# First stage's last group worked batch by batch, its one-hot matrices made earlier, and a context transpose given two more PSUM banks

## The chip, the cores and the metric

The kernel runs on one NeuronCore of a Trainium2 chip. The metric is the device time of one execution in microseconds (us). PE is TensorE, DVE is VectorE, ACT is ScalarE, POOL is GpSimd and SP is SyncE. PE's sequencer, like each of the others, takes its instructions in the order in which the program has them, so an instruction that waits for a semaphore holds up all that stand behind it on that engine.

## The reference, cut to what matters

Six layers, each followed by a residual addition and a layer norm, on 8 batches of 256 tokens of 256 features:

```python
x = _layernorm(x + L0_attn(x))            # 16 heads of 64, causal
x = _layernorm(x + L0_xattn(x, ctx))      # one head, 120 context rows, weights = softmax(q @ ctx.T + mask)
x = _layernorm(x + L0_ffn(x))             # 8 experts, the best 2 of each token, softmax of the 2 gates
x = _layernorm(x + L1_attn(x))            # 16 heads of 16, gated, then an MLP
x = _layernorm(x + L1_xattn(x, ctx))      # 4 heads of 64 on 120 context rows
x = _layernorm(x + L1_ffn(x))             # token shift, receptance, squared relu
```

## The kernel before, in words

A "tile" is 128 tokens. The 16 tiles are worked in G = 4 groups g of NT = 4 tiles, that is GB = 2 batches of 256 tokens. SBUF is one tensor (`words` in the profile) and PSUM another (`bank`, 8 banks of 512 floats), so the profile's names tell a space only; lines tell the operation. Order and semaphores are written by hand for each engine. There are three blocks of code with a barrier between them.

**First stage** (`attention_layers`, lines 165 to 771): the first attention, the first context attention, the gate and the routing. A group has 16 units (batch, pair of heads), and each unit goes round the engines: scores on PE (`unit_scores`, L369), maximum on DVE (L691, L695), exponential on ACT (L571), reciprocal of the sum on DVE (L700), multiplication on POOL (L324), transposes on PE (`unit_turn`, L382) three units later, copy on DVE (L706), value product on PE (`unit_heads`, L395) four units later, copy to `zt` on ACT (L579). Then comes the group's tail: output product (L505, four tiles), residual and statistics (L709, L108, L110), the power on POOL (L128, L130, `norm_rstd`), the normalised rows (L120), their transposes (L406, copied by ACT L559), query product (`tail_queries`, L414), logits (L425), maximum (L723), exponential (L591), transposes of the weights (L435), context sums (L443), the same statistics and rows again for the second norm, its transposes, the gate product (`tail_gate`, L452), the choice of the two experts on DVE (L739 to L748, `choose` L620 to L626), the count on PE (`count`, L462, L463, L466) and the rank in the expert's list (`rank`, L634 to L647). For groups 0 to 2 this tail is interleaved with the projection of the next group (`project`, L358). Group 3 has no next group, and its tail stands alone.

**Table of sources.** Every (tile, choice) pair n = 0 to 31 has two one-hot matrices of 128x128, the "low" (L313) and the "high" (L315), made by POOL from the ranks (`one_hot`), the last eight high ones by DVE (L765). PE multiplies each pair into one accumulating bank (`place`, L477). There are OH = 8 buffers, which lie over the buffers of the unit loop, so that none is made before the last unit of group 3 is done. From the count DVE also works out columns (`columns`, L653 to L675), and a last product (L540) gives the list of rows per slot tile (L771). The three first experts' weights are loaded by SP when the last unit has left (`load_expert`); the rest in the second stage.

**Second stage** (`expert_layer`, to line 1003): 39 slot tiles. POOL gathers the rows (L829) and copies half the expert's up weights (L842), ACT copies the other half (`copy_weights`, L935) and the transposed rows (`copy_rows`, L920) and takes the sigmoid (L924). PE transposes (L870), multiplies up (L886) and down (L897).

**Last stage** (`last_layers`): the three last layers as a pipeline of periods. In period p the front works group a = p, the middle r = p - 1, the rear z = p - 2; periods 2 and 3 have all three. In the rear, `context_turn` (L1424) transposes the softmaxed context weights of a tile into a bank, `context_copy` (L1937, ACT) takes them out, `context_sums` (L1435, copied by ACT L1981) multiplies by the values, `context_product` (L1335, banks 6 and 7 by turns) is added by DVE (`add_product`, L2343). All `product` calls have line 1335. In the periods `context_turn` used bank 1 for all four tiles:

```python
def context_turn(g, t, banks=(1,), sm=sm):
    if t >= len(banks):
        pe.wait_ge(xtc, NT * g + t - len(banks) + 1)
```

## Time and profile before

| | us |
|---|---|
| median of 3 runs | 1292.29 (1290.97 to 1292.76) |
| the profiled execution's own time | 1291.66 |
| its span, from the first to the last instruction | 1289.9 |
| PE busy in the span | 1125.7 (87%) |
| DVE busy | 743.0 (58%) |
| ACT busy | 543.1 (42%) |
| POOL busy | 456.0 (35%) |
| mean granted TensorE clock | 0.951 of full speed |

All positions below are us from the span's start. The first stage ends at about 522, the second at about 750. A time line's row has the start, the time from the first start to the last end of the merged instructions, engine, line and operation, the output and its inputs, the number of records (a float32 product is two records on PE), and in brackets how long the engine had been idle before and what released it.

### The profile page before, as it was taken

What the parts mean: (1) busy time and instruction counts of PE and PEld (TensorE: products, weight loads), DVE (VectorE), ACT (ScalarE), POOL (GpSimd) and SP (SyncE); (2) the same over time, 40 slices, a digit from 0 to 9 for tenths busy, and PEclk for the clock granted to TensorE, in tenths of its full rate; (3) what the DMA queues carried; (4) which work ended last, traced back from release to release, by engine and by line L of the source; (5) the groups of instructions that cost most, each with busy time, mean ns of one, the idle gap of its engine ahead of it and who ended that gap; (6) DMA issues with size and microseconds to landing.
All of it is one profiled execution on the core that took longest, in us unless ns stands there. A gap on an engine that the chain in (4) does not pass through costs nothing. (4 is left out here: it accounts for less than half of the span.)

```text
span 1289.9 us, 20369 instructions
## 1 busy us (share of the span) xinstructions
PE 1125.7 (87%) x6738; PEld 794.2 (62%) x6738; DVE 743.0 (58%) x2247; ACT 543.1 (42%) x1409; POOL 456.0 (35%) x531
## 2 busy tenths in 40 slices
PE   7889988998899886799999937788898898889996
PEld 3456446644654565799999925554654575466775
DVE  1482376347524844455656536758748577756366
ACT  1371246126421721233333317466465457443541
POOL 0150035004300557666666541524322422232122
PEclk9999999999999998799999969589998999899998
DMA  6000110020001040651111132100000100000001
GB/s 194 17 1 1 46 27 2 1 56 17 1 1 56 2 158 19 221 182 51 50 50 47 43 119 64 33 1 25 10 8 1 34 9 17 1 1 25 1 1 33
DMA packets 40228, 52.38 MB, mean 41 GB/s; under 512 B 10780, under 2 KB 33372, under 8 KB 40124
## 3 DMA queue, kind: packets, MB, share of 16 engines
q1 hardware_dynamic: 31100, 36.66, 8.9%
q0 software_dynamic: 3408, 9.31, 2.6%
q10 hardware_dynamic: 5616, 5.11, 1.2%
q8 instruction: 55, 0.90, 0.3%
q14 instruction: 49, 0.40, 0.1%
HBM read 41.76 MB, written 9.31 MB: 40 GB/s over the span
## 5 line engine op out<-in xcount | busy, mean ns | idle before, releaser
L1335 PE MATMUL bank<-words 128*128 128x256 f32 (+3 forms) x872 | 275.4, 467 | 20.9 <-ACT words L1921 5.7
L1335 PEld LDWEIGHTS bank<-words 128*128 128x128 f32 (+1 forms) x872 | 164.8, 196 | 105.5 <-issue 58.9
L358 PE MATMUL bank<-words 128*128 128x512 f32 x384 | 172.7, 601 | 8.3 <-DMA words<-in_wq 8.3
L324 POOL TENSOR_TENSOR words<-words 128x256 f32<-128x256 f32 (+1 forms) x128 | 103.6, 831 | 189.9 <-DVE words L700 189.9
L886 PEld LDWEIGHTS bank<-words 128*128 128x128 f32 x1248 | 147.6, 194 | 4.3 <-ACT words L920 2.4
L886 PE MATMUL bank<-words 128*128 128x128 f32 x1248 | 148.1, 278 | 1.7 <-ACT words L920 1.7
L571 ACT ACTIVATE words<-words 128x128 f32<-128x128 f32 (+1 forms) x256 | 113.3, 444 | 50.0 <-DVE words L695 50.0
L358 PEld LDWEIGHTS bank<-words 128*128 128x128 f32 x384 | 72.3, 192 | 90.4 <-issue 89.8
L553 ACT ACTIVATE words<-bank 128x512 f32<-128x512 f32 x48 | 28.7, 598 | 192.1 <-PE bank L358 192.1
L935 ACT ACTIVATE words<-words 128x1024 f32 x39 | 41.2, 1057 | 146.3 <-PE bank L886 120.8
L610 DVE COPY words<-bank 128x512 f32<-128x512 f32 x48 | 33.2, 691 | 105.8 <-PE bank L358 105.6
L691 DVE CUSTOM_DVE_ANT_0 words<-bank,words 128x128 f32<-128x128 f32 (+1 forms) x256 | 76.0, 354 | 20.5 <-PE bank L369 18.9
L897 PE MATMUL bank<-words 128*128 x312 | 73.9, 380 | 0.7 <-DVE words L984 0.7
L382 PE MATMUL bank<-words 128*128 128x128 f32 x384 | 55.8, 282 | 16.8 <-DVE words L706 9.1
L369 PE MATMUL bank<-words 64*128 64x128 f32 (+1 forms) x512 | 58.9, 351 | 8.6 <-DVE words L695 5.2
L395 PE MATMUL bank<-words 128*64 128x256 f32 (+1 forms) x512 | 55.7, 337 | 10.5 <-ACT words L579 9.4
L382 PEld LDWEIGHTS bank<-words 128*128 128x128 f32 x384 | 41.5, 143 | 38.0 <-issue 30.3
L706 DVE COPY words<-bank 128x768 f32<-128x768 f32 x64 | 59.7, 932 | 8.3 <-PE bank L382 8.3
L1228 POOL TENSOR_TENSOR words<-words 128x2 f32<-128x2 f32 x32 | 7.0, 218 | 162.0 <-DVE words L2353 161.9
L842 POOL COPY words<-words 128x1024 f32 x39 | 40.4, 1037 | 61.4 <-PE bank L886 61.4
L1993 ACT ACTIVATE words<-bank 128x768 f32<-128x768 f32 x64 | 48.9, 811 | 29.3 <-DVE bank L2445 29.2
L128 POOL TENSOR_TENSOR words<-words 128x4 f32<-128x4 f32 x8 | 1.6, 203 | 167.3 <-DVE words L110 167.3
(301 smaller groups left out, 2051.2 us busy)
## 6 DMA issues: line engine op xcount, KB each, us to landing
words<-in_w SPq DMA_DIRECT2D x8, 1024.0 KB, 12.3
y_slots<-words ACTq DMA_DIRECT2D x39, 128.0 KB, 1.7
words<-in_w SPq DMA_DIRECT2D x8, 512.0 KB, 12.6
words<-in_xt SPq DMA_DIRECT2D x4, 512.0 KB, 3.7
words<-in_x SPq DMA_DIRECT2D x4, 512.0 KB, 4.2
x_rows<-words SPq DMA_DIRECT2D x16, 128.0 KB, 1.8
words<-in_wm SPq DMA_DIRECT2D x2, 1024.0 KB, 6.5
out_x<-words SPq DMA_DIRECT2D x16, 128.0 KB, 1.8
```

Source lines behind the costliest of these rows:

```text
L324: last = pool.tensor_tensor(part, part, inv[:, j % SLOTS0, :, t:t + 1].to_broadcast([P, 2, P * (t + 1)]), ALU.mult)
L358: last = pe.matmul(bank[c % 2][:, :], w, r, start=k == 0, stop=k == KD - 1)
L369: last = pe.matmul(bank[SCORES[i % 2][n]][:, t * P:t * P + P * (t + 1)],  kt[r, m, b * S + t * P:b * S + (t + 1) * P], qt[r, m, b * S:b * ...
L382: last = pe.transpose(bank[2 + n][:, k * P:(k + 1) * P], prob[:, j % SLOTS0, n, c:c + P], ident[:, :])
L395: last = pe.matmul(bank[4 + j % 2][DH0 * n:DH0 * n + DH0, queries], v[:, 2 * b + k, h * DH0:(h + 1) * DH0], probt[:, j % 2, n, probs_of], ...
L571: last = act.activation(prob[:, i % SLOTS0, n, c], prob[:, i % SLOTS0, n, c], ACT.Exp, bias=negmax[:, i % SLOTS0, n, t:t + 1], scale=DH0 * ...
L691: dve.tensor_tensor_reduce(out=prob[:, i % SLOTS0, n, c], in0=bank[SCORES[i % 2][n]][:, c], in1=mask0[:, c], scale=1.0, scalar=-3e38, op0= ...
L706: dve.tensor_copy(probt[:, j % 2, :, :], turned).then_inc(tcopied, 1)
L886: last = pe.matmul(bank[(BANKG, BANKV)[half][j % 2]][:, c * P:(c + 1) * P], wfix[:, j % 2, k * 2 * FF + half * FF + c * P:k * 2 * FF + hal ...
L897: last = pe.matmul(bank[BANKY[j % 2]][:, 0:D], hidden[:, j % 2, k * P:(k + 1) * P], w2[:, bass.ds(e * W2 + k * D, D)], start=k == 0, stop= ...
L1335: last = pe.matmul(out, w, r, start=i == 0, stop=i == len(pairs) - 1)
L1993: act.activation(es[:, j % 4, :, :], pair(j % 2)[:, :, 0:CAUSAL], ACT.Exp, scale=DH1 ** -0.5).then_inc(s1e, 1)
```

## The change

Four things are changed.

1. The last group's tail in the first stage is worked by batches of two tiles, b = 0 and 1, with functions of its own on each engine (`last_output`, `last_turn`, `last_queries` and so on). Two of the four output products and the first transposes stand inside the end of the unit loop; the steps of batch 0 stand between those of batch 1.
2. The one-hot matrices get more room: 4 of the 32 pairs in a buffer of their own (`firsthots`), 8 over `wv` (free once the last projection is done), 4 over `xt`, and 8 (`latehots`) over the unit loop's buffers. POOL makes the first four in group 2's units (one in four units), the next eight in group 3's (one in two units). The last count is split in two, so 4 pairs instead of 8 depend on it alone. Since expert 2's weights lie over `wv`, their load waits for the 12th placement and stands behind the stores of the group's rows on SP.
3. In the second stage ACT copies the second slot tile's weights before the first tile's rows, no longer after the first sigmoid.
4. In periods 2 and 3 of the last stage the context weights of tiles 2 and 3 are transposed into banks 6 and 7, after the fourth query/key product; the first two MLP products (`up`) stand ahead of the four context sums, no longer between them.

```diff
+        latehots = cut(turning, 0, (OH, 2, P))
+        firsthots = sb([P, OH // 2, 2, P])
+        weighthots = wv[:, :, :].rearrange("p k (h r n) -> p (k h) r n", r=2, n=P)
+        tokenhots = xt[:, :, :].rearrange("p k (h r n) -> p (k h) r n", r=2, n=P)
...
-                    for e in range(EARLY):
+                    for e in range(EARLY - 1):
                         load_expert(sp, dram, keep, e)
...
+            sp.wait_ge(placed, OH + OH // 2)
+            load_expert(sp, dram, keep, EARLY - 1)
             sp.wait_ge(rowsout, 16 * NT * G)
...
+                    if g == FINAL - 1 and j % 4 == 0:
+                        pool.wait_ge(ranked, 1)
+                        one_hot(j // 4)
+                    if g == FINAL and j % 2 == 0:
+                        pool.wait_ge(ranked, 2)
+                        one_hot(OH // 2 + j // 2)
...
+            one_hot(OH + 4)
+            one_hot(OH + 5)
+            last_rstd(n1, 0)
+            one_hot(OH + 6)
+            one_hot(OH + 7)
+            pool.wait_ge(ranked, G - 1)
+            pool.wait_ge(heads, UNITS * G)
+            for n in range(2 * OH, 2 * OH + 6):
                 one_hot(n)
+            last_rstd(n1, 1)
+            one_hot(2 * OH + 6)
+            one_hot(2 * OH + 7)
+            last_rstd(n2, 0)
+            last_rstd(n2, 1)
             pool.wait_ge(ranked, G)
-            for n in range(3 * OH, 4 * OH):
+            for n in range(3 * OH, 3 * OH + OH // 2):
+                one_hot(n)
+            pool.wait_ge(ranked, G + 1)
+            for n in range(3 * OH + OH // 2, 4 * OH):
                 one_hot(n, both_parts=False)
...
+                    if g == FINAL and i == UNITS:
+                        pe.wait_ge(zcopied, UNITS * g + PAIRS0)
+                        pe.wait_ge(shifted, UNITS * g + UNITS - 1)
+                        last_output(0)
+                        last_output(1)
+                    if g == FINAL and i == UNITS + 2:
+                        pe.wait_ge(shifted, UNITS * g + UNITS)
+                        last_turn(n1, 0, lambda t: x1[:, t, :], TURNED1[0])
...
+            last_queries(0)
+            pe.wait_ge(zcopied, UNITS * G)
+            pe.wait_ge(tcopied, UNITS * G)
+            last_output(2)
+            pe.wait_ge(loaded, 16 * LOADS * G)
+            last_logits(0)
+            last_output(3)
+            last_weights(0)
+            last_sums(0)
+            place(0, OH)
+            last_turn(n1, 1, lambda t: x1[:, t, :], TURNED1[1])
+            place(OH, OH + OH // 2)
+            last_queries(1)
+            last_logits(1)
+            last_turn(n2, 0, lambda t: x2(FINAL, t), TURNED2[0])
+            last_gate(0)
+            last_weights(1)
+            last_sums(1)
+            place(OH + OH // 2, 2 * OH)
+            last_count(0)
+            place(2 * OH, 3 * OH)
+            last_turn(n2, 1, lambda t: x2(FINAL, t), TURNED2[1])
+            last_gate(1)
+            last_count(1)
+            place(3 * OH, 4 * OH)
...
+            last_output(2)
+            last_max(0)
+            last_output(3)
+            last_rows(n1, 1, lambda t: x1[:, t, :])
+            last_sums(0)
+            last_rows(n2, 0, lambda t: x2(FINAL, t))
+            last_max(1)
+            last_gate(0)
+            choose(FINAL, 0)
+            last_sums(1)
+            rank(FINAL, 0)
+            last_rows(n2, 1, lambda t: x2(FINAL, t))
+            last_shares(0)
+            last_gate(1)
+            choose(FINAL, 1)
+            rank(FINAL, 1)
+            for n in range(4 * OH - OH // 2, 4 * OH):
...
             copy_weights(0)
+            copy_weights(1)
             copy_rows(0)
             sigmoid(0)
-            copy_weights(1)
             copy_rows(1)
...
                 if z is not None:
-                    context_turn(z, 2)
-                    context_turn(z, 3)
-                    pe.wait_ge(xtc, NT * z + NT)
+                    pe.wait_ge(xtc, NT * z + HALF)
                 if a is not None:
                     queries_keys(a, 3)
...
                 if z is not None:
                     pe.wait_ge(xe, GB * z + GB)
-                for q in range(GB * KD):
-                    if z is not None:
+                    context_turn(z, 2, (6, 7))
+                    context_turn(z, 3, (6, 7))
+                if r is not None:
+                    for c in range(2):
+                        pe.wait_ge(vcop, NT * a + c + 3)
+                        up(r, c)
+                if z is not None:
+                    pe.wait_ge(xtc, NT * z + NT)
+                    for q in range(GB * KD):
                         context_sums(z, q)
```

PE at the end of the first stage before: the last value products of the unit loop (L395), all four output products (L505), then each step for four tiles.

```order
L395 MATMUL bank<-words 64x128 x2
L505 MATMUL bank<-words 128x256 x32
L477 MATMUL bank<-words 128x128 x8
L406 MATMUL bank<-words 128x128 x8
L414 MATMUL bank<-words 128x512 x4
L425 MATMUL bank<-words 128x120 x8
L435 MATMUL bank<-words 120x128 x4
```

PE at the same place in the changed kernel, from the last value product of the loop (L456). L558 is the query product, L542 an output product, L567 logits, L575 transposes of weights, L582 context sums, L535 placements, L550 row transposes.

```order
L456 MATMUL bank<-words 64x128 x2
L558 MATMUL bank<-words 128x256 x4
L542 MATMUL bank<-words 128x256 x8
L567 MATMUL bank<-words 128x120 x4
L542 MATMUL bank<-words 128x256 x8
L575 MATMUL bank<-words 120x128 x2
L582 MATMUL bank<-words 128x256 x2
L535 MATMUL bank<-words 128x128 x8
L550 MATMUL bank<-words 128x128 x4
L535 MATMUL bank<-words 128x128 x4
L558 MATMUL bank<-words 128x256 x4
```

Batch 0 has its queries, logits, weights and sums between the output products of batch 1, and the first 12 placements stand around the transposes of batch 1.

PE in the context attention of period 2 before: transposes (L1424), the products (L1335, of which the 512-wide pair ahead of the first sums is the fourth query/key product and the next two are `up`), sums (L1435).

```order
L1335 MATMUL bank<-words 128x512 x2
L1335 MATMUL bank<-words 128x256 x4
L1424 MATMUL bank<-words 120x128 x8
L1335 MATMUL bank<-words 128x512 x2
L1435 MATMUL bank<-words 64x128 x4
L1335 MATMUL bank<-words 128x512 x2
L1435 MATMUL bank<-words 64x128 x4
L1335 MATMUL bank<-words 128x512 x2
L1435 MATMUL bank<-words 64x128 x8
```

The same place in the changed kernel (L1631 products, L1720 transposes, L1731 sums):

```order
L1631 MATMUL bank<-words 128x256 x4
L1631 MATMUL bank<-words 128x512 x2
L1720 MATMUL bank<-words 120x128 x8
L1631 MATMUL bank<-words 128x512 x4
L1731 MATMUL bank<-words 64x128 x16
```

The fourth query/key product has moved ahead of the last two transposes, and all four sums stand together behind both `up` products.

## Rows read from the trace of the kernel before

**Rows 1.** Windows view: stretch, length, PE, PEld, DVE, ACT, POOL busy, PEclk, DMA.

```profile
466.60:522.30 55.70, 43.67 (x204) 35.15 (x204) 24.25 (x102) 6.77 (x23) 40.80 (x60) 0.84 0.30 102
```

**Rows 2.** Time line of PE, end of the first stage.

```profile
457.90 0.87 PE L395 MATMUL bank<-words 128*64 128x256 f32 x8
...
467.03 14.08 PE L505 MATMUL bank<-words 128*128 128x256 f32 x64 [0.48 <-ACT words L579]
...
480.95 1.95 PE L477 MATMUL bank<-words 128*128 128x128 f32 x16
...
486.58 3.70 PE L414 MATMUL bank<-words 128*128 128x512 f32 x8 [0.47 <-ACT words L559]
...
491.18 1.12 PE L425 MATMUL bank<-words 128*128 128x120 f32 x8 [0.89 <-issue]
...
504.83 3.25 PE L452 MATMUL bank<-words 128*128 128x8 f32 x16
```

**Rows 3.** Time line of DVE, end of the first stage.

```profile
500.00 0.45 DVE L733 SCALAR_TENSOR_TENSOR words<-bank,words 128x256 f32<-128x256 f32 x1
...
501.04 0.18 DVE L110 BATCH_NORM_AGGREGATE words<-words 128x2 f32<-128x6 f32 x1
...
502.72 1.44 DVE L120 TENSOR_SCALAR words<-words 128x256 f32<-128x256 f32 x4 [1.50 <-POOL words L130]
...
508.11 0.19 DVE L739 COPY words<-bank 128x32 f32<-128x32 f32 x1 [3.95 <-PE bank L452]
...
513.17 0.28 DVE L634 TENSOR_TENSOR words<-words,bank 128x32 f32<-128x32 f32 x2 [0.87 <-PE bank L466]
...
514.94 2.44 DVE L765 TENSOR_SCALAR words<-words 128x128 f32<-128x128 f32 x8
...
522.07 0.20 DVE L771 CAST words<-bank 128x39 int32<-128x39 f32 x1 [0.74 <-PE bank L540]
```

**Rows 4.** Time line of POOL, units of group 3 and a one-hot.

```profile
447.75 1.62 POOL L324 TENSOR_TENSOR words<-words 128x256 f32<-128x256 f32 x2 [1.45 <-DVE words L700]
...
450.22 1.62 POOL L324 TENSOR_TENSOR words<-words 128x256 f32<-128x256 f32 x2 [0.85 <-DVE words L700]
...
503.32 1.02 POOL L315 TENSOR_SCALAR words<-words 128x128 f32<-128x128 f32 x1
```

**Rows 5.** Groups by line, POOL's one-hots: busy us, mean ns, idle before.

```profile
L313 POOL TENSOR_SCALAR words<-words 128x128 f32<-128x128 f32 x32 | 19.6, 619 | 5.3 <-PE bank L395 4.3 <-DVEq L648 1.0
...
L315 POOL TENSOR_SCALAR words<-words 128x128 f32<-128x128 f32 x24 | 19.5, 814 | 0.0
```

**Rows 6.** Time lines of PE and ACT at the start of the second stage.

```profile
535.12 3.84 PE L886 MATMUL bank<-words 128*128 128x128 f32 x32 [1.25 <-ACT words L920]
...
533.74 1.06 ACT L935 ACTIVATE words<-words 128x1024 f32 x1 [0.17 <-issue]
```

**Rows 7.** Time line of PE, context attention of periods 2 and 3.

```profile
977.35 0.65 PE L1424 MATMUL bank<-words 128*120 128x128 f32 x4 [1.75 <-DVE words L2410]
...
980.09 3.78 PE L1335 MATMUL bank<-words 128*128 128x512 f32 x4 [0.69 <-ACT words L1937]
...
1001.43 3.71 PE L1335 MATMUL bank<-words 128*128 128x512 f32 x8 [2.67 <-ACT words L1921]
...
1121.86 5.40 PE L1335 MATMUL bank<-words 128*128 128x512 f32 x8 [2.99 <-ACT words L1921]
```

**Rows 8.** Time line of DVE, the same stretches.

```profile
989.61 1.34 DVE L2648 TENSOR_SCALAR words<-words 128x128 f32<-128x128 f32 x1
...
992.84 0.42 DVE L2343 TENSOR_TENSOR words<-bank,words 128x256 f32<-128x256 f32 x1 [1.89 <-PE bank L1335]
...
1112.95 0.42 DVE L2343 TENSOR_TENSOR words<-bank,words 128x256 f32<-128x256 f32 x1 [1.73 <-PE bank L1335]
```

**Rows 9.** Windows view while PE ran the rows at 980.09 and 1121.86.

```profile
980.00:982.00 2.00, 1.91 (x3) 0.87 (x4) 2.00 (x2) 0.04 (x1) 0.50 (x1) 0.50 0.00 0
...
1124.00:1128.00 4.00, 4.00 (x14) 1.92 (x13) 0.00 (x0) 0.27 (x1) 0.00 (x0) 0.72 0.00 0
```

More of the change, by code:

```diff
@@ L469, in place @@
-            def place(first, number=OH):
-                for n in range(first, first + number):
+                pe.matmul(bank[3][:, 0:NT * NE], ones[:, :], running[:, NT * g:NT * (g + 1), :].rearrange("p t e -> p (t e)"),
+                          start=False, stop=True).then_inc(counted, 1)
+            def place(first, last):
+                for n in range(first, last):
                     pe.wait_ge(hotlow, n + 1)
-                    if n < 3 * OH:
+                    if n < 4 * OH - OH // 2:
@@ L651, in columns @@
             def columns():
[L653 removed]
+                dve.tensor_scalar(length[:, :], bank[SUMMED[1]][:, HALF0 * NE:HALF0 * NE + NE], (P - 1) / 2, 1 / P, ALU.add, ALU.mult)
                 dve.drain()
@@ new lines, in last_shares @@
+            def last_shares(b):
+                h, tiles = slice(HALF0 * b, HALF0 * b + HALF0), slice(NT * FINAL + HALF0 * b, NT * FINAL + HALF0 * b + HALF0)
+                first, second = (keep["weight"][:, tiles, r] for r in range(2))
+                dve.wait_ge(gexp, FINAL + b + 1)
+                dve.tensor_scalar(gq[:, h], ge[:, h], 1.0, None, ALU.add)
+                dve.drain()
+                dve.reciprocal(first, gq[:, h])
+                dve.drain()
+                dve.tensor_tensor(second, first, ge[:, h], ALU.mult)
```

281 lines of the change are left out of this document (215 added, 66 removed).

## Prediction

> **What bounds the kernel now.** All positions are us of the profiled execution, whose span is 1289.9 and whose own time is 1291.66, 0.63 under the median of the three runs, 1292.29. I read the windows view first, to see where no engine is full, then the time lines of PE, DVE and POOL there, for who waits for whom. From the last value product of the first stage to its end lie 55.7 us [rows 1]. PE is busy for 43.67 of them and POOL for 40.80, neither is full, and the granted clock averages 0.84. It is a serial chain: 14.08 us of output products before any normalised row can be turned, then a chain of steps each of which takes four tiles [rows 2, 3]. That chain is the first place of the change.
>
> The second is the start of the second stage, where PE waits 1.25 us for ACT, which was in a 1.06 us weight copy [rows 6].
>
> The third is the context attention of periods 2 and 3. PE shows gaps around its transposes, but DVE works without a gap up to the end of L2648 (989.61 + 1.34 = 990.95) and only then waits, 1.89 us for the first context product, in period 3 1.73 us [rows 7, 8]. Since DVE's next result feeds ACT's last exponential, its table load and the gelu for which PE waits at 1001.43, this DVE wait bounds the place, not PE's gaps.
>
> **End of the first stage.** The work is the same but for order, so I walk the new order with the old durations.
>
> PE leaves the heads of the twelfth unit at 457.90 + 0.87 = 458.8 [rows 2]. Now two output products of 14.08 / 4 = 3.52 each follow, to 465.8, in time that used to be the loop's draining. Then come seven steps of units (three turns, four heads) of 0.87 each, eight turn records (about 1.0) and some 0.5 of waits for DVE's copies: 473.4. Queries for one batch cost 3.70 / 2 = 1.85, output product three 3.5, logits of one batch 1.1 (the row at 491.18 is for two tiles), the last output product 3.5 [rows 2]. It ends at 483.4, while before it ended at 467.03 + 14.08 = 481.1.
>
> From there to the last statistics of the second norm took 20.1 before (481.1 to 501.04 + 0.18 = 501.2) for four tiles. For two tiles I take off 1.85 of queries, 0.7 of turning, 1.3 of the four maxima and exponentials, and 2.3 for two of the four statistics, which stand 1.2 apart (500.00 to 501.22) [rows 3]: 14.0. I add what now stands between: up to 2.0 for placements (eight take 1.95 [rows 2]) and context sums ahead of batch 1's turn, 0.9 for the turn and gate of batch 0 on PE, 0.8 for gate and choice of batch 0 on DVE. That makes 17.7, so 501.1: by then nothing has been won, since the later output products have eaten it.
>
> After that the halves pay. Before, from 501.2: 1.50 for POOL's power, rows at 502.72, gate on DVE at 508.11, the count read at 513.17, high one-hots 514.94 to 517.38, end at 522.07 + 0.20 = 522.27 [rows 3]. Now DVE ranks batch 0 while POOL works, to 502.9; two rows (half of 1.44), one turn, one copy and a gate product of 3.25 / 2 = 1.6 (at the low clock of that row; about 1.0 at the high one) bring the gate to 506.2, so 1.9 less. Gate and choice handle half the width: 0.7 less. The count saves 0 to 0.7 by the clock; I take 0.2. Four high one-hots instead of eight save half of 2.44, 1.2. Columns, table and last product stay. The sum is 4.0: **the stage ends at 518.3**. Bounds: 3.2 if the clock is low all along, 4.9 if it stays high, and 1.5 more or less for the 501.1.
>
> POOL's one-hots: a pair costs 0.62 + 0.81 = 1.43 [rows 5]. Twelve pairs move into the units. Two units use 2 x 1.62 of POOL and leave 1.45 + 0.85 idle, a period of 5.54 [rows 4]; with one pair more POOL is at 4.67 of it. After a pair the next multiplication can be late by 1.43 - 0.85 = 0.58, but PE reads it only three units after its scores, so I cost it at nothing. If that cover were gone, see the rivals. Pairs 12 to 23 are made while POOL would wait: the six before the second power of the first norm (8.6 us from the heads at 473.4) end near 482, and tile 3's statistics come at 484.6. Expert 2's load now starts near 504, behind two row stores on SP, and is not used before the slot tiles of experts 0 and 1 are done, so it costs nothing.
>
> **Second stage.** ACT copies the second tile's weights before the rows arrive, when it is idle. The row copy that PE waits for then starts right behind PE's transposes instead of behind the rest of a 1.06 us copy [rows 6]. Of the 1.25 us wait some 0.45 remain for the row copy itself: 0.8 won. Nothing, if ACT's copy were late for the first rows, is the lower bound.
>
> **Context attention.** PE no longer waits between transposes 977.35 and 980.09 [rows 7], and the first context product is ready by about 987. DVE then starts at 990.95, and 1.89 and 1.73 are the most that can be won [rows 8]. But PE, ahead by then, idles some four us, since the third product waits for DVE's first addition. The row at 980.09 shows what follows short work with gaps: four records take 3.78, where eight take 3.71 in the row at 1001.43, and the granted clock is 0.50 [rows 7, 9]. If the clock falls to its lower level (1.2 GHz of 2.4) at that point, products three and four are late by about 1.2 and `up` by more, and 0.5 of the 1.89 remains. In period 3 the same fall now hits the two `up` products behind the gelu: 5.40 where period 2 has 3.71, at a granted clock of 0.72 [rows 7, 9]; with PE busy before, that 1.7 should go. So 0.5 and 0.5 + 1.7: **2.7 us**; between 0 and 3.6 + 1.7.
>
> The Trainium skill (TensorE: Matmul & The Clock Gate, What's actually happening) states that the clock is passed at one of two ratios, set by how busy PE has been recently. The granted 0.50 and the row of 3.78 agree; by that rule a PE that gets ahead and then idles loses part of its lead, and by the row alone I would have taken the full 3.6.
>
> **Sum.** 4.0 + 0.8 + 2.7 = 7.5. Against the median: 1292.3 - 7.5 = **1284.8**.
>
> **Rivals.**
> - *The clock holds.* PE stays at the high level through the end of the first stage (+0.9) and the context products (+0.9). For: PE is denser than before in both. Against: 0.84 in the stretch before [rows 1], and PE still waits for DVE. 9.3 won, 1283.0.
> - *Interleaving costs more.* Each engine runs both batches in one queue, so one late step of batch 0 (its rows wait for POOL, its gate for PE) holds batch 1. If three such waits of 1 us hit the chain, the first stage gives 1.0 and the whole 4.5: 1287.8. For: DVE has 16 steps of the two batches in one queue. Against: I found each input ready but for about 1 us.
> - *The context part gives nothing*, because PE's lost clock eats it: 4.8 won, 1287.5.
> - *One-hots hold the units: slower.* They share POOL with the multiplications on which the turns rest. It decides where a one-hot pair takes over 5.54 - 3.24 = 2.30 us, or where PE's turns have no slack for 0.58. If all of 12 x 1.43 = 17.2 lay on the path, the kernel would lose 9.7: 1302. For: POOL's high one-hot took 1.02 when DVE's row scaling ran beside it, 0.81 on average [rows 4, 5]. Against: even then a pair is 1.7.
>
>   The Trainium skill (SBUF — State Buffer, Who interferes with whom) has a rule that speaks against this: GpSimd and a VectorE instruction of a two-port mode take turns on one port pair, and the later one waits for the whole instruction. By it, DVE's small scalings between units would be held by up to a one-hot each, 12 x 0.81 = 9.7, and the kernel would be 2.2 slower if none of that were hidden. The trace agrees only with a wait on POOL's side: DVE's four rows took 1.44 beside the slowed one-hots [rows 3, 4].
>
> **Chances.** Forecast 0.50, clock holds 0.20, interleaving 0.14, context nothing 0.08, one-hots hold the units 0.04, the rest (an expert's load or a barrier that hides all) 0.04. 0.2%, 2.6 us, is about what a measurement of this kernel can tell from no change. The first four, 0.92, are all faster by more, and I take 0.02 off for small gains; 0.06 for within and 0.04 for slower. The range reaches from the clock rival with the upper bound of the context part (1292.3 - 11 = 1281.3) to the interleaving rival with the ACT term gone (1292.3 - 3.5 = 1288.8).
>
> **What would show it.** The last CAST of the first stage at 518.3 instead of 522.07 + 0.20, with the last statistics of the second norm near 501 and the last output product's end near 483.4; the unit loop's period unchanged at 5.54 per two units and no PE wait for POOL's L371; no wait of PE before the second slot tile's products above 0.5; DVE's first context addition directly behind its scaling of the squares in periods 2 and 3, and the gelu release 0.5 to 1.9 us earlier in the stage's own time. It would be wrong if the units' period grew, if the chain between 483 and 501 took over 20, or if periods 2 and 3 kept their length.

## The result, and the profile after

The changed kernel takes 1287.22 us (median of 20 runs, 1281.88 to 1293.22), the kernel before 1292.5 us (20 runs, 1290.67 to 1296.24). The ratio is 0.9955, its 95% interval 0.9945 to 0.9965: **5.8 us faster, 4.5 to 7.1**. The profiled execution took 1288.51 us, with a span of 1286.8 and a mean granted clock of 0.949, against 0.951 before.

**End of the first stage.** Time line of PE in the changed kernel, as in [rows 2]. L542 is an output product, L550 a transpose, L558 the query product, L535 a placement, L590 the gate:

```profile
460.12 7.17 PE L542 MATMUL bank<-words 128*128 128x256 f32 x32
...
480.46 3.63 PE L542 MATMUL bank<-words 128*128 128x256 f32 x16
...
485.75 1.95 PE L535 MATMUL bank<-words 128*128 128x128 f32 x16
487.53 0.60 PE L550 MATMUL bank<-words 128*128 128x128 f32 x4
...
503.83 1.06 PE L590 MATMUL bank<-words 128*128 128x8 f32 x8 [0.69 <-ACT words L718]
```

The two early output products stand inside the unit loop, and the last one ends at 480.46 + 3.63 = 484.1. Time line of DVE, as in [rows 3]: rows of the first norm of batch 1, last statistics of the second norm, high one-hots, end of the stage.

```profile
486.51 0.79 DVE L899 TENSOR_SCALAR words<-words 128x256 f32<-128x256 f32 x2 [1.19 <-POOL words L363]
...
500.05 0.18 DVE L882 BATCH_NORM_AGGREGATE words<-words 128x2 f32<-128x6 f32 x1
...
510.57 1.28 DVE L1060 TENSOR_SCALAR words<-words 128x128 f32<-128x128 f32 x4
...
516.84 0.20 DVE L1067 CAST words<-bank 128x39 int32<-128x39 f32 x1 [0.19 <-PE bank L693]
```

The stage ends at 517.04, 5.2 before the 522.27 of [rows 3]. But group 3's units began at 418.69 in this execution and at 417.67 in the one before: the first unit began 1.19 earlier here, but group 0 then took 2.08 longer, in code that both kernels share. From there to the end it took 104.60 before and takes 98.35: **6.25 won in the tail**. In the time frame of the kernel before, 1.02 is to be taken off every position above.

These are two single executions, and the one before was a quick one. Two experiments below (ACT's order only, context part only) have the old code in this stage, and it took 106.85 and 106.86 in their profiles. The first difference is the query product, 3.70 before [rows 2], here in ACT's order only:

```profile
486.09 5.40 PE L414 MATMUL bank<-words 128*128 128x512 f32 x8 [0.47 <-ACT words L559]
```

The new code took 98.1 to 99.2 in the eight profiles that have it without a change to its one-hots. So the tail wins between 5.4 and 8.8 us by profiles.

**Units with one-hots in them.** Groups by line, PE's transposes from the start of group 3's units to the last heads (about 56 us), first the kernel before, then the changed one:

```profile
L382 PE MATMUL bank<-words 128*128 128x128 f32 x96 | 13.8, 280 | 4.7 <-DVE words L706 2.6 <-POOL words L324 1.5
```

```profile
L443 PE MATMUL bank<-words 128*128 128x128 f32 x96 | 13.7, 279 | 4.5 <-DVE words L983 2.6 <-POOL words L371 1.5
```

The wait for POOL's multiplications is 1.5 us with and without one-hots between them. The units are a little slower all the same: from the first score product of group 3 to its last it is 39.12 us before and in the three experiments without one-hots there, and 39.5 in the changed kernel and in the seven others with eight pairs. In the changed kernel two units take 5.88 instead of 5.53 at one place, and 5.53 from there on.

**Start of the second stage**, time line of PE, as in [rows 6]: L1166 transposes the gathered rows, L1182 multiplies up.

```profile
522.28 5.90 PE L1182 MATMUL bank<-words 128*128 128x128 f32 x32 [0.47 <-ACT words L1216]
...
528.88 3.84 PE L1182 MATMUL bank<-words 128*128 128x128 f32 x32 [0.47 <-ACT words L1216]
534.05 0.44 PE L1166 MATMUL bank<-words 128*128 128x128 f32 x2 [1.33 <-DMA words<-x_rows,words]
```

ACT's wait fell from 1.25 to 0.47, as forecast. Behind it a new one of 1.33 appeared, for the gathered rows of the third slot tile. From the end of the first stage to the third tile's transposes it is 534.05 - 517.04 = 17.0 us, and it was 538.80 - 522.27 = 16.5 before: this stretch became 0.5 longer.

**Context attention**, time line of PE, as in [rows 7]: the first two context products, then the third and fourth (8 records of 256 columns, merged in the second row with the 8 records of `up` 2 and 3), then the two `up` products behind the gelu, in period 2 and in period 3.

```profile
985.00 1.99 PE L1631 MATMUL bank<-words 128*128 128x256 f32 x8 [0.47 <-ACT words L2277]
991.57 8.44 PE L1631 MATMUL bank<-words 128*128 128x256 f32 x16 [4.57 <-DVE words L2639]
1001.14 3.71 PE L1631 MATMUL bank<-words 128*128 128x512 f32 x8 [1.13 <-ACT words L2217]
...
1121.26 3.71 PE L1631 MATMUL bank<-words 128*128 128x512 f32 x8 [1.46 <-ACT words L2217]
```

DVE's first and fourth context additions of period 2 and the first of period 3, as in [rows 8]:

```profile
991.11 0.41 DVE L2639 TENSOR_TENSOR words<-bank,words 128x256 f32<-128x256 f32 x1
...
995.39 0.42 DVE L2639 TENSOR_TENSOR words<-bank,words 128x256 f32<-128x256 f32 x1 [0.76 <-PE bank L1631]
...
1111.22 0.41 DVE L2639 TENSOR_TENSOR words<-bank,words 128x256 f32<-128x256 f32 x1
```

DVE no longer waits for the first product. PE, ahead, idles 4.57 us and comes back slow. Windows view of those slices (all engines; the last three numbers are the granted clock and the DMA's share and rate):

```profile
990.00:994.00 4.00, 2.43 (x6) 1.98 (x7) 3.26 (x8) 2.63 (x5) 1.68 (x3) 0.61 0.00 0
994.00:998.00 4.00, 4.00 (x8) 2.08 (x7) 2.89 (x8) 1.12 (x2) 1.45 (x3) 0.54 0.00 0
```

**Where the rest is.** The same instruction can be found in every kernel's trace. The table is worked out from the time lines of DVE: how many us later than in the changed kernel an instruction starts, at six of the changed kernel's positions. 600 and 850 lie behind the start of the second stage and in the last stage's first period, 969 is the beginning of period 2's context attention, 1008 behind its gelu, 1128.5 the same in period 3. Where a number changes from one column to the next, time was lost or won between.

| profile of | 600 | 850 | 969 | 1008 | 1128.5 | 1280 |
|---|---|---|---|---|---|---|
| before | 4.7 | 3.5 | 0.1 | 0.3 | 2.3 | 3.1 |
| tail only | -1.1 | -2.2 | -2.8 | -1.9 | 0.1 | 0.0 |
| ACT's order only | 6.5 | 5.3 | 1.9 | 2.1 | 4.0 | 4.0 |
| context part only | 6.3 | 5.1 | 1.8 | 1.4 | 1.0 | 2.4 |
| up products between | -0.7 | -0.4 | -1.1 | -0.4 | -0.4 | 1.3 |
| kept warm | -1.8 | -3.2 | -6.5 | -6.3 | -7.8 | -7.8 |
| loads held | -0.8 | -2.2 | -5.6 | -5.6 | -6.3 | -4.7 |
| one-hots twice | 8.4 | 8.6 | 8.0 | 8.0 | 8.0 | 11.2 |
| one-hots late | 18.0 | 16.7 | 13.4 | 13.4 | 12.6 | 15.4 |
| gap filled | 1.3 | 1.0 | 0.9 | 1.1 | 1.3 | 2.9 |
| both filled | -2.0 | -3.5 | -6.9 | -8.3 | -9.4 | -9.4 |
| warm and held | -0.2 | -1.3 | -1.9 | -1.7 | -1.5 | 0.1 |

Against the changed kernel, "before" is 4.7 behind at 600 and level at 969: **4.6 us of the win were lost again in code that the change does not touch**, all of it between 840 and 970. The windows view shows what the clock did there, between 882 and 958. First the kernel before, then the changed one (PE's busy time, the granted clock and the DMA's share and rate), then tail only (busy time of all engines, then the same three):

```profile
898.00:902.00 4.00, 3.30 (x16) 0.63 0.36 100
...
926.00:930.00 4.00, 2.09 (x32) 0.72 0.00 0
930.00:934.00 4.00, 3.91 (x52) 1.00 0.00 0
```

```profile
894.00:898.00 4.00, 3.23 (x16) 0.66 0.36 103
898.00:902.00 4.00, 3.42 (x20) 0.50 0.39 117
...
926.00:930.00 4.00, 2.11 (x33) 0.93 0.00 0
930.00:934.00 4.00, 3.94 (x25) 0.65 0.00 0
```

```profile
918.00:922.00 4.00, 2.72 (x32) 1.52 (x32) 3.37 (x17) 1.16 (x3) 0.10 (x1) 0.69 0.00 0
922.00:926.00 4.00, 1.98 (x20) 1.41 (x24) 2.65 (x7) 1.75 (x3) 3.05 (x5) 0.50 0.00 0
926.00:930.00 4.00, 4.00 (x24) 2.85 (x16) 2.32 (x6) 2.16 (x4) 0.24 (x1) 0.53 0.00 0
```

Before, one slice has PE at work at a low clock (898 to 902), and the other low one, 926 to 930, is half idle. In the changed kernel there are three with PE at work, one of them at 0.50; in tail only PE is busy through 926 to 930 at 0.53. Not every execution of the new tail pays this: kept warm, loads held and both filled have the same code there (loads held but for one wait of SP), are 5.5 to 6.7 ahead of "before" at 600 and 5.7 to 7.0 at 969, and one-hots late loses nothing there either. The other six with the new tail (the changed kernel, tail only, up products between, gap filled, warm and held, one-hots twice) lose 2.9 to 4.6, and the two with the old tail nothing. The runs fit that: the changed kernel's 20 times lie between 1281.9 and 1293.2, twice the spread of before.

### The profile page after: what moved, and what is told of

It is laid out like the page before. It is cut to its first block and busy times, and to the rows that moved or that the text cites. A ratio compares the mean times of both kernels' runs of the same rounds, so it can differ in the third digit from the quotient of the medians.

```text
span 1286.8 us, 20425 instructions
## 1 busy us (share of the span) xinstructions
PE 1123.6 (87%) x6750; PEld 796.0 (62%) x6750; DVE 743.7 (58%) x2260; ACT 544.2 (42%) x1407; POOL 459.7 (36%) x539
## 5 line engine op out<-in xcount | busy, mean ns | idle before, releaser
L1631 PE MATMUL bank<-words 128*128 128x256 f32 (+3 forms) x872 | 276.1, 469 | 26.7 <-DVE words L2639 9.1
L1631 PEld LDWEIGHTS bank<-words 128*128 128x128 f32 (+1 forms) x872 | 166.7, 198 | 112.7 <-issue 58.0
L1182 PEld LDWEIGHTS bank<-words 128*128 128x128 f32 x1248 | 147.4, 194 | 3.5 <-ACT words L1216 1.6
L1182 PE MATMUL bank<-words 128*128 128x128 f32 x1248 | 147.9, 277 | 0.9 <-ACT words L1216 0.9
L808 DVE COPY words<-bank 128x512 f32<-128x512 f32 x48 | 33.2, 691 | 104.6 <-PE bank L419 104.3
L456 PE MATMUL bank<-words 128*64 128x256 f32 (+1 forms) x512 | 56.4, 340 | 10.0 <-ACT words L762 9.0
L2741 DVE TENSOR_TENSOR bank<-bank,words 128x512 f32<-128x512 f32 x64 | 42.0, 694 | 32.9 <-PE bank L1686 32.6
```

What stands on the lines that cost most here:

```text
L456: last = pe.matmul(bank[4 + j % 2][DH0 * n:DH0 * n + DH0, queries], v[:, 2 * b + k, h * DH0:(h + 1) * DH0], probt[:, j % 2, n, probs_of], ...
L1182: last = pe.matmul(bank[(BANKG, BANKV)[half][j % 2]][:, c * P:(c + 1) * P], wfix[:, j % 2, k * 2 * FF + half * FF + c * P:k * 2 * FF + hal ...
L1631: last = pe.matmul(out, w, r, start=i == 0, stop=i == len(pairs) - 1)
L2741: dve.tensor_tensor(diagonal, diagonal, mask1[:, :].unsqueeze(1).to_broadcast([P, 4, P]), ALU.min).then_inc(s1m, 1)
```

## Experiments

The ratios are against the kernel before, run on the same chip: 1293.47 us (25 runs) for the three parts and up products between, 1292.83 (18 runs) for kept warm, loads held and the two kernels with other one-hots, 1292.29 (13 runs) for gap filled, both filled and warm and held. A range behind a ratio is its 95% interval.

### The three parts, each alone

**Tail only**: the changed kernel with ACT's order and the context part put back.

> The kernel before with the batchwise end of the first stage, the early one-hots and expert 2's late load alone; ACT's order in the second stage and the context transposes are as before. In the profile of the whole change this stage ended 6.25 us earlier, counted from the start of group 3's units (98.35 against 104.60), where the prediction had 4.0. Theory: that is the tail's own and is kept to the end, so 98.3 to 98.4 from the units' start and 5.5 to 6.5 us less in all. Rival, that part of it is PE's clock falling luckily in that profile: 99.5 to 101 here, and 4 us or less in all. PE's wait for the third slot tile's rows (the gather) stays at 0 in both, as ACT's order is the old one.

Measured: 1288.69 us (7 runs), ratio 0.9963 (0.9949 to 0.9977), **4.8 won, 3.0 to 6.6**, which holds both the 5.5 to 6.5 of the theory and the rival's 4. From the units' start to the end of the stage its profile has 99.2, which is neither's. Its second stage missed the forecast too: the third tile's transposes wait 0.43 for the gather, with ACT's order still the old one, and the wait for ACT is 0.60 where it was 1.25. Its profile is 5.8 ahead of before at 600 and 5.7 at 850. By 1008 only 2.2 of that are left: the rest was lost in the last stage, whose code is the same in both.

**ACT's order only**: the kernel before with `copy_weights(1)` moved up.

> The kernel before with ACT's second weight copy ahead of its first row copy alone. In the profile of the whole change the second slot tile's products began 0.94 us earlier, but PE then waited 1.33 us for the rows of the third slot tile. Theory: the gather of the third tile is issued at the same time as before and lands about 8.7 us later, because the experts' loads fill the DMA engines, so whatever ACT wins is waited away there: 0 us, with a PE wait of about 0.9 before the third tile's transposes. Rival, that the wait belongs to the whole change (expert 2's load moved): 0.8 to 0.9 us less and no such wait.

Measured: 1292.95 us (11 runs), ratio 0.9992 (0.9984 to 1.0001): 1.0 won, between -0.1 and 2.1, so the times alone tell 0.8 from nothing as little as from twice as much. The time line of PE tells more:

```profile
536.11 3.84 PE L886 MATMUL bank<-words 128*128 128x128 f32 x32 [0.47 <-ACT words L920]
540.59 0.44 PE L870 MATMUL bank<-words 128*128 128x128 f32 x2 [0.64 <-DMA words<-x_rows,words]
```

The wait is 0.47 instead of 1.25, and the next transposes, which before followed without a gap, wait 0.64 for the gather. Against the frame of the units, the second tile's products came 0.8 earlier and the third's at the old place. What ACT gave, the gather took: from the end of the first stage to the third tile's transposes it is 16.55, and 16.53 before.

**Context part only**: the kernel before with the new PE order and banks of periods 2 and 3.

> The kernel before with the context transposes of tiles 2 and 3 in banks 6 and 7 alone. Prediction: DVE's first addition 1.89 and 1.73 us earlier in periods 2 and 3, most of it lost in period 2 because the clock falls while PE idles and the third and fourth products are late; in period 3 the products behind the gelu take 3.7 instead of 5.4. That gives 0 to 0.5 for period 2 and 2.2 for period 3, 2.2 to 2.7 in all. Rival, that the clock is not the cause: both periods keep 1.7 to 1.9, 3.6 in all.

Measured: 1289.7 us (10 runs), ratio 0.9976 (0.9967 to 0.9985), **3.1 won, 1.9 to 4.3**. By the table it is 1.6 to 1.8 behind "before" at 600, 850 and 969 (its units began 0.66 earlier, and the end of the first stage, with the old code and the query product of 5.40, then took 2.26 longer) and 0.7 ahead at 1280: 2.4 in its profile. The first addition of period 2 came 1.98 earlier against the instructions just ahead of it, the fourth only 0.55. The table's step from 969 to 1128.5 is +2.2 in "before" and -0.8 here, so 3.0 by then, some of which goes again at the end.

By their medians the three parts add to 4.8 + 1.0 + 3.1 = 8.9, and the whole gives 5.8; with half-widths of 1.8, 1.1 and 1.2 the intervals overlap.

### PE ahead and idle: can the context products be used better?

**Up products between**: in periods 2 and 3,

```diff
-                    for t in range(NT):
-                        context_product(z, t)
+                    context_product(z, 0)
+                    context_product(z, 1)
...
+                    up(r, 2)
+                    up(r, 3)
...
+                    context_product(z, 2)
+                    context_product(z, 3)
...
-                    for c in range(2, 6):
-                        up(r, c)
+                    up(r, 4)
+                    up(r, 5)
```

> The whole change, and in the periods with a context attention the MLP products up 2 and up 3 stand between the second and the third context product, where PE idles about four us for DVE's first addition. Theory: PE works through that time, the clock stays at its upper level, products three and four take under 1 us each, and period 2 keeps the whole 1.9 us of DVE's earlier start: 1.3 to 1.9 us less than the whole change, most of it in period 2. Rival, that DVE's additions are bound by something else: no change, or up to 1 us more because the third product now waits behind up 3.

Measured: 1289.71 us (9 runs), ratio 0.9967 (0.9954 to 0.9981), no better than the whole change, where 1.3 to 1.9 less was expected. DVE's additions came earlier, but PE then had nothing before the gelu:

```profile
990.42 1.99 PE L1631 MATMUL bank<-words 128*128 128x256 f32 x8 [1.13 <-DVE words L2645]
998.53 3.78 PE L1631 MATMUL bank<-words 128*128 128x512 f32 x4 [6.11 <-ACT words L2223]
```

Four records took 3.78 (and all eight 5.90) where eight take 3.71 in the changed kernel. The gap had only been moved.

**Kept warm**: the same, and behind the fourth context product four products of 512 columns whose result nobody reads (L1968).

```diff
+                    pe.wait_ge(turning, NT * a + NT)
+                    for i in range(4):
+                        pe.matmul(bank[3][:, :], wm1[:, 0, tok(i)], h5t[:, 0, :], start=True, stop=True)
```

> The order of ups_between (up 2 and up 3 ahead of the third context product) with four 512-wide products more behind the fourth context product, whose result nobody reads, in the time in which PE waits for the first gelu (6.11 us in ups_between in both periods). Theory, that PE's idle time there costs the clock: the two products behind the gelu take 3.7 us instead of 5.90 and 5.22, the added products (0.93 each at the upper level, 3.7 us) lie inside the wait, and the kernel is 2.5 to 4 us faster than ups_between, that is 1.5 to 3 us faster than the whole change. Rival, that the clock does not depend on PE's own work there: 5.2 to 5.9 as before and no gain, or a loss if the added products hold up 4.

Measured: 1281.23 us (7 runs, 1280.28 to 1291.44), ratio 0.9932 (0.9908 to 0.9955), 8.8 won. Periods 2 and 3:

```profile
986.86 3.60 PE L1968 MATMUL bank<-words 128*128 128x512 f32 x8
993.14 5.40 PE L1631 MATMUL bank<-words 128*128 128x512 f32 x8 [2.68 <-ACT words L2226]
```

```profile
1107.19 3.60 PE L1968 MATMUL bank<-words 128*128 128x512 f32 x8
1113.47 3.71 PE L1631 MATMUL bank<-words 128*128 128x512 f32 x8 [2.68 <-ACT words L2226]
```

The same filler and the same 2.68 of idle time gave a slow pair in one period and a quick one in the other. In the stage itself the table gives 1.3 us (from -6.5 to -7.8). The other 6.5 that its profile is ahead were there at 969, before the edit acts, so **the median of this kernel is better by more than the edit explains**: five of its seven runs lie at 1280.3 to 1282.8 and two at 1287.7 and 1291.4.

**Gap filled** puts those four products where PE idles 4.57 us in the changed kernel, between the second and the third context product, in the order of the change (into the bank of `up` 2). **Both filled** has them and three more ahead of the wait for the gelu.

> The whole change, with four products of 512 columns whose result nobody reads put between the second and the third context product of periods 2 and 3, where TensorE idles 4.57 us for VectorE's first addition. Theory (the clock falls in that gap): the third and fourth context products run at the high clock, VectorE's fourth addition comes about 1.4 us earlier against the first one (2.8 after it instead of 4.3) in both periods, so 2.8 won; but TensorE then idles some 2.7 us before the gelu and the two products behind it take 5.40 instead of 3.71, which gives 0 to 3.4 back. Total between 3 us faster than the whole change and the same. Rival (the gap costs nothing, the clock falls by itself): the products behind the gap are as slow as before, the additions stand where they stood, and the time is the whole change's.

Measured for gap filled: 1288.07 us (8 runs), ratio 0.9959 (0.9945 to 0.9974), the same as the whole change. Its time line of PE:

```profile
987.73 3.60 PE L1960 MATMUL bank<-words 128*128 128x512 f32 x8
992.46 5.43 PE L1631 MATMUL bank<-words 128*128 128x256 f32 x16 [1.13 <-DVE words L2644]
1000.57 5.40 PE L1631 MATMUL bank<-words 128*128 128x512 f32 x8 [2.68 <-ACT words L2222]
```

The same 16 records take 5.43 here and 8.44 in the changed kernel: that is what 4.57 of idle time cost, 3.0 us (in period 3 it is 5.43 and 8.11). DVE's fourth addition comes 2.83 behind the first, not 4.28. And PE, done sooner, idles 2.68 before the gelu, after which the `up` pair takes 5.40 and not 3.71. From 969 to 1128.5 the table moves by 0.4. Both halves of the theory are seen, and they cancel.

> As the kernel with the products in the gap, and three more such products ahead of the wait for the gelu. Theory: both idle stretches are filled, so the additions come 1.4 us earlier in each period and the products behind the gelu stay at 3.71: 2.8 us less than the whole change, about 1284.5, without the reordering of the up products. Rival (in the kernel kept warm the order of the up products made the gain, not the filling): no faster than the whole change, 1287, or slower by what the added products hold up.

Measured for both filled: 1281.54 us (6 runs, 1279.11 to 1287.47), ratio 0.9929 (0.9911 to 0.9947). Period 2:

```profile
984.71 5.43 PE L1631 MATMUL bank<-words 128*128 128x256 f32 x16 [1.14 <-DVE words L2648]
989.98 2.74 PE L1970 MATMUL bank<-words 128*128 128x512 f32 x6
992.83 3.71 PE L1631 MATMUL bank<-words 128*128 128x512 f32 x8
```

Neither is slow now, in both periods, and the table gives 2.5 from 969 to the end (-6.9 to -9.4), of the 2.8 expected. The median is 5.7 under the whole change's; the rest again lies before 969 in the profile, in code that both share. So one profile shows 2.5 us for the filling, and the runs a median of 1281.5 for this kernel, but not that the filling brings all of the difference.

### The third tile's gather

**Loads held**: SP waits with expert 3's weights until the first two gathers of buffer 0, that of the third tile with them, have landed.

```diff
                     sp.wait_ge(gathered[1], 16)
+                    sp.wait_ge(gathered[0], 32)
```

> The whole change, and SP issues the loads of experts 3 to 5 only after the third slot tile's rows have landed. Theory, that the experts' loads on the DMA engines make the third gather take 8.7 us: it lands some 3 to 5 us earlier, PE's wait of 1.33 us before the third tile's transposes goes, and the kernel is 1.0 to 1.4 us faster than the whole change. Rival, that POOL's issue of the gather is late (it follows two weight copies): the wait stays at 1.3 and nothing changes. A second risk is that the wait comes back at the fourth or fifth tile, whose gathers then meet the loads.

Measured: 1284.91 us (6 runs), ratio 0.9944 (0.9927 to 0.9962), 7.2 won. The third tile has no wait, the fourth a small one:

```profile
532.62 0.38 PE L1167 MATMUL bank<-words 128*128 128x128 f32 x2
...
538.74 0.44 PE L1167 MATMUL bank<-words 128*128 128x128 f32 x2 [0.43 <-DMA words<-x_rows,words]
```

In both kernels with the load held the third tile's wait is gone, and in all seven others with ACT's new order and the new tail it is there, so the load beside the gather is what delays it. But its size differs in the same code: 1.33 in the changed kernel, 1.92 in up products between, 2.54 in gap filled, 0.39 in kept warm and 0.41 in both filled. From the end of the first stage to the transposes of the last slot tile it is 214.8 us with the load held, 215.8 in the changed kernel, and 214.7 in kept warm and both filled, which hold nothing. So the 1.0 between the two profiles, and the 2.3 between the medians, are not shown to be the edit's.

**Warm and held** is kept warm with this edit.

> The kernel kept warm (up products between the context products, four products nobody reads ahead of the gelu) with expert 3's load held until the third tile's rows have landed. If the two savings stand in different places and add: 0.9 to 1.4 us less than the kernel kept warm, about 1280. Rival: the start of the second stage is eaten again before the stage ends by a change of the clock, no difference from it.

Measured: 1285.76 us (6 runs), ratio 0.9944 (0.9925 to 0.9964), **a miss**: the two did not add, and it is no faster than loads held alone. The third tile's wait is gone and the fourth's 0.43 is there. There was nothing to win by that: kept warm's own wait at the third tile was 0.39 in its profile. But both `up` pairs behind the gelu were slow, and from 600 to 969 its profile fell back by 2.9 against "before", where kept warm lost nothing. Its six runs lie in two clumps, 1282.7 to 1283.8 and 1287.8 to 1290.4.

### The one-hots in the units

**One-hots twice**: each of the eight pairs of group 3's units is made twice, with a wait between.

```diff
                         pool.wait_ge(ranked, 2)
+                        again(OH // 2 + j // 2)
+                        pool.drain()
                         one_hot(OH // 2 + j // 2)
```

> The whole change, and in the units of group 3 POOL makes each of the eight one-hot pairs twice. Theory: two units have 5.54 us, POOL needs 2 x 1.62 for them and 1.43 for a pair, and PE reads its result only later, so one pair is hidden (measured: the unit loop of group 3 is 0.4 us longer than before at most), but two are not: 3.24 + 2.86 = 6.10, so 0.56 us more for each of the eight double units, 3 to 5 us in all. Rival, that POOL has more slack than that or that DVE's small operations are held by each one-hot: 0, or over 8 us.

Measured: 1295.45 us (10 runs), ratio 1.0014 (1.0003 to 1.0024). POOL over one period of two units (L377 is the multiplication, L360 begins the extra pair and L352 the one that is kept), and PE's group of transposes:

```profile
446.24 3.19 POOL L377 TENSOR_TENSOR words<-words 128x256 f32<-128x256 f32 x4
449.40 0.61 POOL L360 TENSOR_SCALAR words<-words 128x128 f32<-128x128 f32 x1
...
450.95 0.60 POOL L352 TENSOR_SCALAR words<-words 128x128 f32<-128x128 f32 x1 [0.17 <-issue]
...
452.30 3.19 POOL L377 TENSOR_TENSOR words<-words 128x256 f32<-128x256 f32 x4
```

```profile
L451 PE MATMUL bank<-words 128*128 128x128 f32 x90 | 13.7, 291 | 9.0 <-POOL words L377 8.2 <-DVE words L991 0.8
```

POOL has next to no idle time left, the period is 452.30 - 446.24 = 6.06 instead of 5.53, and PE's wait for it grew from 1.5 to 8.2. The group's score products now take 43.2 us instead of 39.5, so 3.7 more in the loop. The forecast of 3 to 5 in all was missed: the whole lost 7.6 against the changed kernel by the ratios, and in the profiles the stage from the units' start was 7.2 longer (105.5 against 98.35), half of it behind the loop. One pair in two units is hidden but for the 0.4 of the section on the profile, two are not.

**One-hots late**: none is made before the last unit has left; the 24 that were early are made around the powers of the tail.

> The whole change with no one-hot matrix in the units: POOL makes all 24 pairs of groups 0 to 2 after the unit loop, between the powers of the norms. Theory: the batchwise order is only worth something with the early matrices. 24 x 1.43 = 34 us of POOL and four powers end about 512 instead of the last of the 24 at 489, and PE's placements of them stand ahead of the second norm's transposes of batch 1, so the stage ends 8 to 10 us later and the kernel is 2 to 5 us slower than the kernel before. Rival, that the matrices are hidden anyway as they were before: 0 to 2 us later than the whole change.

Measured: 1304.93 us (4 runs), ratio 1.0093 (1.0079 to 1.0108), 12.0 slower than before and some 18 slower than the whole change. PE (L529 is a placement, L544 a row transpose):

```profile
510.49 0.77 PE L529 MATMUL bank<-words 128*128 128x128 f32 x2 [2.71 <-POOL words L354]
...
520.60 1.06 PE L544 MATMUL bank<-words 128*128 128x128 f32 x4
```

and POOL:

```profile
507.90 0.20 POOL L361 TENSOR_TENSOR words<-words 128x2 f32<-128x2 f32 x1 [10.84 <-DVE words L876]
```

I had the direction and not the size: 2 to 5 us slower than before was expected. The third eight pairs stood behind the last power; POOL idled 10.84 us ahead of that, then made one pair every 1.36, and PE's last transposes stood behind the placements. The stage ended at 536.25 instead of 517.04. Where I put those eight pairs matters: at 1.36 each they would have fitted into the 10.84 us in which POOL idled, and PE's last transposes would not have stood behind them. So some 11 of the 18 us (an estimate from these rows) may belong to that choice. That the order by batches wins only with early one-hots is likely, but a kernel with late ones at their best place was not run.

## Why the prediction was right, and where it was not

The forecast was 1284.8 with a range of 1281.3 to 1288.8; 1287.2 came out, 5.8 (4.5 to 7.1) won of 7.5. That the two are near is in part luck: the tail gave more than its share, the second stage nothing, and the clock elsewhere took a part back.

- **Last output product** by 483.4: 483.1 in the frame of before. Right.
- **Last statistics** at 501.1: 499.2, so 1.9 more than forecast, 0.3 of it from the earlier output product. The step that failed is "up to 2.0 for placements (eight take 1.95) and context sums ahead of batch 1's turn". PE did run them from 484.8 to 487.5. But batch 1's rows were being made on POOL and DVE in that time (they begin at 486.51), and the transposes at 487.53 followed at once. The term of 2.0 was too large: I had charged work that lay beside a wait.
- **Behind the statistics** 501.2 to 522.27 before, 21.1; forecast 17.2, measured 517.04 - 500.23 = 16.8. The four high one-hots took 1.28 instead of 2.44, the 1.2 forecast. Right within 0.4.
- The tail in all: 4.0 forecast, bounds 1.7 to 6.4, 6.25 measured in the profile, 4.8 (3.0 to 6.6) by the medians of tail only. Against the old tail's 106.85 it would be 8.5: I walked with 3.70 for a query product that took 5.40 in two of three profiles of that code.
- **One-hots in the units**: "I cost it at nothing" was wrong by 0.4 us, the 39.5 against 39.12 of the group's score products, though PE's wait for POOL is 1.5 with and without them. The rule of the Trainium skill (SBUF — State Buffer, Who interferes with whom), by which a VectorE instruction of a two-port mode waits for all of a GpSimd one that came first, could have cost up to the 9.7 of the prediction. The trace does not show a loss of that size: it is 0.4 in the loop, and the later periods of two units are 5.53 against the 5.54 that I worked with. What did show is a slower one-hot beside DVE's row scaling: 0.66 and 0.86 in the tail at 486.5, 0.60 and 0.79 alone.
- **Second stage**: 0.8 forecast. The wait went as said, but one tile later nothing was left of it in ACT's order only (16.55 against 16.53; the times alone allow 0 to 2), and in the changed kernel 0.5 had been lost (17.0 against 16.5). The failed step is "of the 1.25 us wait some 0.45 remain for the row copy itself: 0.8 won": I did not ask what is late next. It was the third tile's gather. It was issued at 525.29 in the changed kernel and used 8.8 later, while an expert's load ran. In the kernel before it was used 8.6 behind its issue, and PE did not wait for it, being later itself. The new tail alone also had taken half of ACT's wait away (0.60 in tail only).
- **Context part**: 0.5 + 2.2 = 2.7 forecast. Against the instructions just ahead of it (which stand 0.24 later in the changed kernel than before, where the table's column 969, some 20 us ahead of them, still has the changed kernel 0.1 ahead) the first addition of period 2 came 1.98 earlier, and 0.53 of that was left at the fourth addition and behind the gelu. In period 3 the fourth addition came 0.68 earlier and DVE's first instruction behind the gelu 2.37. So 0.5 + 2.4 = 2.9. Alone the part won 3.1 (1.9 to 4.3). The argument held, that PE ahead idles and then runs slow: 8.44 for what takes 5.43 in gap filled. The Trainium skill (TensorE: Matmul & The Clock Gate, What's actually happening) states that the clock follows how busy PE has been. This trace agrees: granted clocks of 0.61 and 0.54 in the slices behind the idle stretch.
- **What no step had**: the clock in code that the change does not touch. In the profiled execution this took back 4.6 us between 840 and 970, where six of ten profiles with the new tail lost 2.9 to 4.6, and it is the likely reason why the parts add to 8.9 and the whole gives 5.8. That is argued from the table and the spread, not shown by an experiment: I made none that fixes the clock there. What decides whether an execution loses these us stays open.

By rivals: of "the clock holds" the opposite happened in the context part and before it; "interleaving costs more" did not, the tail gave more than forecast; "one-hots hold the units" decides where I said, between one pair (1.4 us of the 2.3 free in two units) and two (2.8). The bottom of the range's win, 3.5, is a slip of the sum: 4.5 without ACT's 0.8 is 3.7, so 1288.6. It decides nothing here.

## What to carry to other kernels

When a wait is to be removed, look up what the waiting engine needs next and when that arrives; 0.8 us of ACT went straight to a gather that nobody had waited for. Working a serial tail by halves shortened the part behind the last common step from 21.1 to 16.8 us here; the independent work beside it (24 one-hot pairs) has to be out of the way by then. Such work can be put into another engine's loop almost free while that engine has idle time in its period (one pair in two units cost 0.4 us) and not when it has none (two pairs cost 3.7 more). And an engine that gets ahead only to idle can run its next work at half the clock: price the gap as well as the wait. Old code is no fixed yardstick either: the same tail took 104.6 in one profile and 106.9 in two others. Measure such a change by many runs, not by one profile.

## What I had not expected of the hardware

- Idle time of PE costs more than itself: 4.57 us of it made 16 records take 8.44 instead of 5.43. Useless products in the gap gave that back. But the same 2.68 us of idle time behind the same 3.60 us of filler was followed by 5.40 in period 2 and 3.71 in period 3 of kept warm, so it is not a fixed price.
- A change that makes the kernel faster doubled the spread of its runs (from 5.6 us between the lowest and the highest of 20 to 11.3).
- A gather with an expert's load beside it made PE wait 0.39, 0.41, 1.33, 1.92 or 2.54 us in five profiles of the same code; with the load held back that wait was gone in both.
- POOL's one-hots slowed the group's units by 0.4 us in each of eight profiles, though the time that PE is seen waiting for POOL did not change.
